# Rotating the first matmul's blocks over three PSUM banks, and giving the front turns a third bank

## The reference

```python
x = x + conv_ref(_ln_c(x), fc1_w, fc2_w, sa_w)     # channel gate, then a 7 x 7 spatial gate
t = _to_tokens(x)                                  # 192 tokens of 512 channels per image
t = t + ffn_ref(_ln_t(t), w1, w2)                  # 512 -> 2048 -> 512, both layers "bitlinear"
x = _from_tokens(t, x)

# conv_ref(v): ca = sigmoid(mlp(mean over pixels) + mlp(max over pixels)); v = v * ca
#              s = conv7x7([mean over channels, max over channels]);       return v * sigmoid(s)
# _bitlinear(x, w): w -> clip(round(w * rms), -1, 1) / rms;  x -> round(x * 127 / max|x|) / scale
#                   per token;  then x @ w.T
# ffn_ref: h = gelu(_bitlinear(x, w1)); out = _bitlinear(h, w2)
```

## Time and profile before

| | us |
|---|---|
| median of 3 runs | 321.71 (321.67, 321.71, 323.82) |
| the profiled execution | 321.15 |
| its span, first to last instruction | 319.4 |
| PE busy | 275.2 (86%) |
| DVE busy | 256.8 (80%) |
| ACT busy | 218.0 (68%) |
| POOL busy | 162.4 (51%) |

### The profile page before, as it was taken

The page is one execution under the profiler, slowest core; times in us unless marked ns, Lnnn a source line. Parts: engine busy times, 40 slices in busy tenths (PEclk is TensorE's granted clock), DMA queues, the critical chain, the costliest instruction groups (busy, mean ns, idle before and its releaser), DMA issues.

```text
span 319.4 us, 5840 instructions
## 1 busy us (share of the span) xinstructions
PE 275.2 (86%) x1834; PEld 153.2 (48%) x1834; DVE 256.8 (80%) x590; ACT 218.0 (68%) x442; POOL 162.4 (51%) x256
## 2 busy tenths in 40 slices
PE   3557659696899999999999999989999998899974
PEld 2444534543456355535553556455535553444431
DVE  1757979979698979897989798989997988799510
ACT  2286397578666878687868786858687757577731
POOL 7404355324855385538553855475538552455410
PEclk9999775959799999999999999999999999999999
DMA  4899400002373028402941294128402631263493
GB/s 132 315 382 422 131 1 2 0 0 43 26 167 66 12 57 232 99 19 49 240 92 27 39 230 102 34 36 222 109 19 49 165 69 23 45 164 67 79 218 99
DMA packets 71078, 34.20 MB, mean 107 GB/s; under 512 B 52040, under 2 KB 68424, under 8 KB 70536
## 3 DMA queue, kind: packets, MB, share of 16 engines
q1 hardware_dynamic: 69384, 32.78, 41.0%
q10 hardware_dynamic: 1664, 1.05, 1.2%
HBM read 14.94 MB, written 6.29 MB: 66 GB/s over the span
## 4 chain that ended last, share of the span: by engine, by line
PE 49%; DVE 27%; issue 9%; ACT 6%; POOL 4%; DMA 3%; SPq 1%; ACTq 0%; DVEq 0%; POOLq 0%
PE ps_o L1152 17%; PE ps_h L1141 9%; PE ps_t L1141 8%; DVE amax L842 4%; PE front L1074 3%; PE small L1117 3%; DVE t L815 3%; PE front L1161 2%; ACT junk L520 2%; PE ps_t L1183 2%; DVE st L817 2%; DVE amax L828 2%; DVE w_room L885 2%; DVE pv L782 2%; PE front L1126 1%
## 5 line engine op out<-in xcount | busy, mean ns | idle before, releaser
L1152 PE MATMUL ps_o<-w2T,hq 128*128 128x512 f16 x384 | 92.7, 380 | 1.2 <-DMA hq<-w_raw 1.2
L474 POOL TENSOR_SCALAR w_room<-w_room,q 128x1024 f32<-128x1024 f32 x48 | 59.0, 1241 | 54.6 <-DVE q L852 54.6
L842 DVE TENSOR_REDUCE amax<-w_room 128x1 f32<-128x1024 f32 (+1 forms) x48 | 57.1, 1208 | 2.2 <-ACT w_room L520 2.2
L1141 PE MATMUL ps_h<-w1T,xq 128*128 128x512 f16 x208 | 55.3, 412 | 1.0 <-ACT xq L520 1.0
L1152 PEld LDWEIGHTS ps_o<-w2T,hq 128*128 128x128 f16 x384 | 35.4, 98 | 37.3 <-issue 3.6
L520 ACT ACTIVATE w_raw<-w_room 128x1024 f16<-128x1024 f16 x48 | 50.1, 1048 | 0.6 <-POOL w_room L474 0.6
L520 ACT ACTIVATE w_room<-ps_h,s 128x512 f32<-128x512 f32 x52 | 35.1, 690 | 15.4 <-PE ps_h L1141 14.3
L1141 PE MATMUL ps_t<-w1T,xq 128*128 128x512 f16 x176 | 42.6, 379 | 0.0
L520 ACT ACTIVATE w_room<-ps_t,s 128x512 f32<-128x512 f32 x44 | 30.3, 688 | 7.7 <-PE ps_t L1141 7.6
L1141 PEld LDWEIGHTS ps_h<-w1T,xq 128*128 128x128 f16 x208 | 20.2, 105 | 25.1 <-issue 6.4
L520 ACT ACTIVATE junk_m<-front 128x192 bf16<-128x192 f32 x64 | 20.5, 331 | 16.2 <-DVE pooled L757 16.2
(11 more groups left out here) (125 smaller groups left out, 458.3 us busy)
## 6 DMA issues: line engine op xcount, KB each, us to landing
out<-w_room SPq DMA_DIRECT2D x16, 384.0 KB, 3.3
x_in<-in_x SPq DMA_DIRECT2D x14, 384.0 KB, 5.3
w_room<-in_L_ffn_w SPq DMA_DIRECT2D x4, 1024.0 KB, 8.9
w_raw<-in_L_ffn_w SPq DMA_DIRECT2D x4, 1024.0 KB, 12.1
x_in<-in_x ACTq DMA_DIRECT2D x2, 384.0 KB, 3.7
hq<-w_raw SPq DMA_TRANSPOSE x48, 3.2
fc_raw<-in_L_conv_fc_w ACTq DMA_DIRECT2D x2, 128.0 KB, 4.1
taps_rev<-in_L_conv_sa_w SPq DMA_DIRECT2D x2, 0.2 KB
```

Source lines behind the costliest of these rows:

```text
L474: pool.tensor_scalar(part, part, q2[tile.par][:, 0:1], MAGIC, ALU.mult, ALU.add).then_inc(g_rounded, 1)
L842: chain.mark(dve.tensor_reduce(amax2[:, i:i + 1], w1_room[:, first + i * F // 2:first + (i + 1) * F // 2 + i], AX.X, ALU.max, apply_absolu ...
L1141: last = pe.matmul(banks[b], xq[tile.pair.par][:, tile.s, k, :], w1T[:, k, b * 512:(b + 1) * 512], start=(k == 0), stop=(k == NC - 1))
L1152: last = pe.matmul(ps_o[:, :], hq[tile.par][:, k, :], w2T[:, k, :], start=(k == 0), stop=(k == NF - 1))
```

## The change

The four blocks of `ffn_in` go over three banks, `ps_h0`, `ps_h1` and `ps_t0`: the block with running number n = 4 * tile + b takes bank n % 3 (from tile 2 on; the first two tiles still use `ps_h0` and `ps_h1` alone). Block b of a tile now waits for `g_ready` of 4 * tile + b - 2, which is the gelu of three blocks earlier. For b = 3 this is the gelu of block 0 of the same tile. `ps_t1` becomes the third `front` bank. The lists `a` and `b` become `free[0]`, `free[1]`, `free[2]`, which carry over from round to round, and the tables say which of the three banks a turn takes. The order of the work on each engine stays as it was; what changes is the bank and the waits.

```diff
@@ -146,13 +146,18 @@
         ps_h = [pb(f"ps_h{i}", [P, 512]) for i in range(2)]
         ps_t = [pb(f"ps_t{i}", [P, 1024], f16) for i in range(2)]
         ps_o = pb("ps_o", [P, 512])
-        front = [pb(f"front{i}", [P, 512]) for i in range(2)]
+        front = [pb(f"front{i}", [P, 512])[:, :] for i in range(2)]
+        front.append(ps_t[1][:, :].bitcast(f32))
         small = pb("small", [P, 512])
-        front16 = [b[:, :].bitcast(f16) for b in front]
+        front16 = [b.bitcast(f16) for b in front]
         h_start = [ps_h[0][:, :], ps_h[1][:, :], ps_h[0][:, :], ps_h[1][:, :]]
-        h_loop = [ps_h[0][:, :], ps_h[1][:, :], ps_t[0][:, :].bitcast(f32), ps_t[1][:, :].bitcast(f32)]
+        h_loop = [ps_h[0][:, :], ps_h[1][:, :], ps_t[0][:, :].bitcast(f32)]
+
+        def h_bank(tile, b):
+
+            return h_start[b] if tile.at() < 2 else h_loop[tile.at(FB, b) % 3]
         fc1_ps = small[0:J, 16:20]
         fc2_ps = small[:, 32:32 + 2 * NC].rearrange("p (k i) -> p k i", i=2)
@@ -307,7 +312,7 @@
             return raw[:, 4 * i:4 * i + 4, :] if k == 0 else raw[:, i, :]
-        OUT_BANK, V1_BANK, XQ_BANK, X_BANK, CA_BANK = [0, 1, 0], [1, 0, 0, 0], [1, 1, 0], [0, 1, 1], [0, 1, 1]
+        OUT_BANK, V1_BANK, XQ_BANK, X_BANK, CA_BANK = [0, 2, 0], [1, 2, 1, 0], [0, 1, 2], [2, 0, 0], [1, 2, 1]
         def wait_all(eng, pairs):
             for semaphore, value in pairs:
                 wait(eng, semaphore, value)
...
@@ -564,14 +569,14 @@
                 copy(xq[tile.pair.par][:, tile.s, :, :],
                      front16[bank][:, 0:C].rearrange("p (k q) -> p k q", k=NC), xq_ready, bias=-F16_ZERO)
-            def gelu(tile, gate=None, banks=h_loop, blocks=range(FB)):
+            def gelu(tile, gate=None, blocks=range(FB)):
                 wait(act, s1_ready, tile.at(1, 1))
                 for b in blocks:
                     if b == 0 and gate:
                         gate_tokens(gate)
                     wait(act, h_done, tile.at(FB, b + 1))
-                    copy(g[tile.par][:, b * 512:(b + 1) * 512], banks[b], g_ready, ACT.Gelu,
+                    copy(g[tile.par][:, b * 512:(b + 1) * 512], h_bank(tile, b), g_ready, ACT.Gelu,
                          scale=s1[tile.pair.par][:, tile.s:tile.s + 1])
             def pack_g(tile, out_tile=None, out_bank=None, halves=range(2)):
...
@@ -1127,18 +1132,13 @@
                 last.then_inc(xq_turned, 1)
                 return [(xq_ready, tile.at(1, 1))]
-            def ffn_in(tile, banks=h_loop, blocks=range(FB)):
+            def ffn_in(tile, blocks=range(FB)):
                 wait(pe, xq_ready, tile.at(1, 1))
-
-                if banks is h_start:
-                    before = [-1, 0, 1, 2]
-                else:
-                    before = [-1, 0, 0, 0] if tile.at() == 2 else [-3, -2, -1, 0]
                 for b in blocks:
-                    wait(pe, g_ready, tile.at(FB, before[b]))
+                    wait(pe, g_ready, tile.at(FB, b - 1 if tile.at() < 2 else b - 2))
                     for k in range(NC):
-                        last = pe.matmul(banks[b], xq[tile.pair.par][:, tile.s, k, :],
+                        last = pe.matmul(h_bank(tile, b), xq[tile.pair.par][:, tile.s, k, :],
                                          w1T[:, k, b * 512:(b + 1) * 512], start=(k == 0), stop=(k == NC - 1))
                     last.then_inc(h_done, 1)
...
@@ -1270,49 +1270,61 @@
             a = turn_x(Tile(pair2, 2), 0, a)
             conv(pair1)
+            free = [a, b, []]
+
             def body(pair, attend, normalise, turn):
                 nxt, att, fresh = pair.plus(1), pair.plus(2), pair.plus(3)
-                a = [(xq_ready, pair.at(NT, NT))]
-                b = [(xt_ready, att.at(NT, NT))] if attend else [(scaled, NP * NT), (out_ready, pair.at(NT, -2))]
-                if attend:
-                    a = a + b
+                def res_out(tile, bank):
+                    free[bank] = turn_res(tile, bank, free[bank])
+
+                def channels(n):
+                    free[V1_BANK[n]] = turn_v1(att, n, V1_BANK[n], free[V1_BANK[n]])
+
+                def quantised(n):
+                    free[XQ_BANK[n]] = turn_xq(Tile(nxt, n), XQ_BANK[n], free[XQ_BANK[n]])
+
+                def tokens(n):
+                    free[X_BANK[n]] = turn_x(Tile(fresh, n), X_BANK[n], free[X_BANK[n]])
+
+                def gate(n):
+                    free[CA_BANK[n]] = spread_ca(Tile(att, n), CA_BANK[n], free[CA_BANK[n]])
                 ffn_in(Tile(pair, 2))
                 if pair.c > 0:
-                    a = turn_res(Tile(pair.plus(-1), 2), OUT_BANK[0], a)
-                if attend:
-                    b = turn_v1(att, 0, V1_BANK[0], b)
+                    res_out(Tile(pair.plus(-1), 2), OUT_BANK[0])
+                if attend:
+                    channels(0)
                 ffn_out(Tile(pair, 0), (0, 1))
                 if attend:
-                    a = turn_v1(att, 1, V1_BANK[1], a)
+                    channels(1)
                 ffn_out(Tile(pair, 0), (2,))
                 if normalise:
-                    b = turn_xq(Tile(nxt, 0), XQ_BANK[0], b)
+                    quantised(0)
                 ffn_out(Tile(pair, 0), (3,))
                 if attend:
-                    a = turn_v1(att, 2, V1_BANK[2], a)
+                    channels(2)
                 if normalise:
                     ffn_in(Tile(nxt, 0))
-                b = turn_res(Tile(pair, 0), OUT_BANK[1], b)
-                if attend:
-                    a = turn_v1(att, 3, V1_BANK[3], a)
+                res_out(Tile(pair, 0), OUT_BANK[1])
+                if attend:
+                    channels(3)
                 ffn_out(Tile(pair, 1), (0, 1))
                 ffn_out(Tile(pair, 1), (2,))
                 if normalise:
-                    b = turn_xq(Tile(nxt, 1), XQ_BANK[1], b)
+                    quantised(1)
                 if attend:
                     fc1(att)
                 ffn_out(Tile(pair, 1), (3,))
                 if attend:
                     if turn:
-                        a = turn_x(Tile(fresh, 0), X_BANK[0], a)
+                        tokens(0)
                     fc2(att)
                     if turn:
-                        b = turn_x(Tile(fresh, 1), X_BANK[1], b)
+                        tokens(1)
                 if normalise:
                     ffn_in(Tile(nxt, 1), blocks=(0, 1, 2))
@@ -1321,24 +1333,24 @@
                 if normalise:
                     ffn_in(Tile(nxt, 1), blocks=(3,))
                 if attend:
-                    a = spread_ca(Tile(att, 0), CA_BANK[0], a)
-                    b = spread_ca(Tile(att, 1), CA_BANK[1], b)
+                    gate(0)
+                    gate(1)
                 ffn_out(Tile(pair, 2), (0,))
-                a = turn_res(Tile(pair, 1), OUT_BANK[2], a)
-                if attend:
-                    b = spread_ca(Tile(att, 2), CA_BANK[2], b)
+                res_out(Tile(pair, 1), OUT_BANK[2])
+                if attend:
+                    gate(2)
                 ffn_out(Tile(pair, 2), (1, 2))
                 if normalise:
-                    a = turn_xq(Tile(nxt, 2), XQ_BANK[2], a)
+                    quantised(2)
                 ffn_out(Tile(pair, 2), (3,))
                 if turn:
-                    b = turn_x(Tile(fresh, 2), X_BANK[2], b)
+                    tokens(2)
                 if attend:
                     conv(att)
             for c in range(NP):
                 body(Pair(c), c < NP - 2, c < NP - 1, c < NP - 3)
-            turn_res(Tile(Pair(NP - 1), 2), OUT_BANK[0], [(out_ready, NP * NT - 1)])
+            turn_res(Tile(Pair(NP - 1), 2), OUT_BANK[0], free[OUT_BANK[0]])
 _INS = ["x", "L0_conv_fc1_w", "L0_conv_fc2_w", "L0_conv_sa_w", "L0_ffn_w1", "L0_ffn_w2"]
```

More of the change, by code:

```diff
@@ L525, in copy_x @@
                 wait(act, q1_ready, tile.at(1, 1 - 2 * NT))
-                copy(xt[tile.pair.par][:, tile.s, :], front[bank][:, :], xt_ready)
+                copy(xt[tile.pair.par][:, tile.s, :], front[bank], xt_ready)
             def token_mean(pair, k, bank):
@@ L594, in copy_out @@
                 copy(out_sb[tile.pair.par][:, :, tile_cols(tile.s)],
-                     front[bank][:, :].rearrange("p (k q) -> p k q", k=NC), out_ready)
+                     front[bank].rearrange("p (k q) -> p k q", k=NC), out_ready)
             def squares(k, raw, loaded, turns):
@@ L637, in _ @@
             squares(1, w2_raw, w2_loaded, (1,))
-            gelu(Tile(pair0, 0), None, h_start, (0, 1))
+            gelu(Tile(pair0, 0), None, (0, 1))
             token_mean(pair1, 1, 1)
             token_mean(pair1, 2, 0)
-            gelu(Tile(pair0, 0), None, h_start, (2, 3))
+            gelu(Tile(pair0, 0), None, (2, 3))
             copy_weights(1, (0,))
@@ L650, in _ @@
             sum_channels(Tile(pair1, 0))
-            gelu(Tile(pair0, 1), None, h_start, (0,))
+            gelu(Tile(pair0, 1), None, (0,))
             sum_channels(Tile(pair1, 1))
```

(20 more changed lines are left out.)

## The result

The changed kernel takes 325.73 us (median of 4 runs, 325.25 to 327.84), the kernel before, beside it, 322.49 us. The ratio is 1.0112 (95% interval 1.0072 to 1.0153). In a later series it was 1.0161 (1.0126 to 1.0195). Forecast were 320.9 us and a range up to 323.2. So the change makes the kernel slower by 1.1 to 1.6%, and the forecast was wrong in sign. Every ratio in this document leaves out runs more than 1.5% above the fastest of their kernel; that is one run, the one of 326.06 us under "Thin fill".

What follows compares the result with a forecast made beforehand. PE and DVE, both nearly full, were taken to bound each round in turn. The profiled 321.15 - 0.36 - 0.4 = 320.4 us; from the median, 321.71 - 0.8 = 320.9 us, range 319.2 to 323.2.

Steps and rivals of the forecast that it cites:

- The bound of a round: Each round is PE from `conv` to the second tile's `ffn_out`, then DVE until `conv`; `conv` stays at 176.42 in round 2.
- the stall that turns into another wait: At the ends of rounds 0 to 5, PE's wait for `copy_out` becomes a 0.9 us wait before `conv`; no gain.
- Three banks for the blocks cost nothing: In `ffn_in`, block 3 waits for its own tile's block 0 gelu, with 0.6 us spare at the tightest; cost 0.
- The 0.36 us of round 4: Mid-round 4, the rounded tile's turn no longer waits for a mean of ACT; gain 0.36 us, bounds 0 and 0.36.
- neither DVE nor POOL is waited for here: Reason given for taking the whole 0.36 us in round 4, nearest to the upper bound.
- The 0.4 us of round 5: In round 5 `res` is turned at once and DVE gets the third gate 0.6 us earlier; gain 0.4 us, bounds 0 and 0.6.
- The clock: Rival: TensorE's clock falls in one `ffn_in` per round, 16 matmuls, costing 20 us over 8 rounds, 341 us; chance 1%.
- 0 of 4.6 us: Value given to removing `turn_xq`'s six waits for `copy_out` at the ends of rounds 0 to 5, since DVE covers them.
- the 0.8 that was forecast: Total gain in us subtracted from the median of 321.71 us; its terms are 0.36 in round 4 and 0.4 in round 5.

Runs made afterwards that it cites:

- Thin fill: The changed kernel with 32 extra 3-column matmuls directly before the convolution of each round with attention; 322.72 us, ratio 1.0011.
- the kernel with that half alone: The kernel before with only the blocks of `ffn_in` moved to three banks, fourth bank unused, front turns on their two banks; 323.34 us, ratio 1.0015.
- the kernel with fill: The changed kernel with four 512-column matmuls, result never read, directly before the convolution of each round with attention; 322.19 us, ratio 0.9983.
- the stall moved without the banks: The kernel before, banks kept, with the turn of a round's last rounded tile moved behind the last quarter of `ffn_out`; 326.09 us, ratio 1.0118.
- the kernel with the stall moved: The kernel before, last rounded tile's turn moved behind `ffn_out`'s last quarter, here with four wide matmuls before the convolution; 321.86 us, ratio 0.9993.
- The kernel with one wait back: The changed kernel with PE again waiting for the output copy before turning a round's last rounded tile; 324.08 us, ratio 1.0048.
- the filled kernel before: The kernel before plus 3 wide matmuls before the last rounded tile's turn (rounds 0-5), 4 and 3 before convolutions of rounds 3 and 5; 321.88 us, ratio 0.9985.

## Why the prediction was wrong

**The bound of a round, and the stall that turns into another wait: right.** `conv` starts when DVE is through; rounds without a fall keep their length, and the wait for `split_stats` stands where it was forecast (about 0.9 us, measured 1.00 in rounds 0 and 1). What failed is the price of that wait, below.

**Three banks for the blocks cost nothing: right** as far as can be told, by the kernel with that half alone.

**The 0.36 us of round 4: the gain came and was given back.** In the kernel with fill, whose round 4 had no fall, `ffn_out`'s result is added at 227.71 and not at 228.11. DVE's timeline there, first this kernel, then the one before:

```profile
227.71 0.75 DVE L864 SCALAR_TENSOR_TENSOR res<-ps_o,s,t 128x512 f32<-128x512 f32 x1
228.38 1.16 DVE L820 SCALAR_TENSOR_TENSOR t<-pv,sg,xt 128x512 f32<-128x512 f32 x1
```

```profile
228.11 0.75 DVE L859 SCALAR_TENSOR_TENSOR res<-ps_o,s,t 128x512 f32<-128x512 f32 x1 [0.27 <-PE ps_o L1152]
228.77 0.81 DVE L815 SCALAR_TENSOR_TENSOR t<-pv,sg,xt 128x512 f32<-128x512 f32 x1
```

The next instruction takes 1.16 against 0.81 us, while POOL rounds in both. The round is 31.49 against 31.50 us. The step "neither DVE nor POOL is waited for here" failed: DVE, come earlier, met POOL's long instruction, and ends 1.66 us behind the start of POOL's work in the one trace and 1.65 in the other. That it is this encounter is read from the two traces and was not tried by itself.

**The 0.4 us of round 5: 0.2 us.** In the same kernel with fill, DVE got the third gate at 267.32 instead of 267.99, as forecast, and then waited 0.35 us for ACT's sum and met POOL's work twice (0.89 and 1.04 us, where two of the four instructions had been slow before). Within the bounds of 0 and 0.6.

**The clock: the step that failed.** The prediction put the wait that moves before `conv` into the sum as "0 of 4.6 us" and gave a fall of the clock 1%, because "longer stalls in one piece before `conv` speak for it, and the same total of stalls speaks against it", and because round 3 had kept its clock. The total alone is the wrong measure. In the kernel before, PE's idle time came in two parts with wide matmuls between them; the change put it in one part, next to the turns and to 1.1 us of 3-column matmuls. About the same sum in one place was followed by a fall in 8 of 18 rounds, shown both ways: the stall moved without the banks gives the loss, and fill at that place takes it away with the banks. The size was also wrong: the rival counted 16 slow matmuls in each of 8 rounds, 20 us. A fall lasts about 3.4 us and costs 1.4 to 1.7 us. Three of them make 4.5 us (1.51, 1.65 and 1.36 us, by the table, the last against the round of the kernel with fill); the spans differ by 4.8. Rounds 1 to 5 together are 4.2 us longer, and near the end of the kernel (at 314.84) PE waits 1.82 us for a transfer of `hq`, where it waited 1.19 before; why that is so is open. The Trainium skill, TensorE: Matmul & The Clock Gate, section A second HAM failure mode: psum-queue depth-cycling, tells of a clock that goes up and down where PE idles briefly between groups of matmuls. The trace of before did not show it, that of the changed kernel does, and the page deserved more than 1%.

**The gain behind it.** Where both kernels have their idle time filled, the change has 320.72 us and the kernel before 321.88, with intervals that don't overlap: 1.2 us, of the size of the 0.8 that was forecast. But the fills are not the same, and with four wide matmuls each, the change (322.19) and the kernel with the stall moved (321.86) show no such gain. So the gain isn't shown.

Open: in which rounds the clock falls. Two traces of the same kernel differ, and stalls of 1.00 us were followed by a fall in one round and not in another. The kernel with one wait back still loses half a per cent at the median; its profiled execution is its fastest run and has the one fall, so that the others are not explained. That the kernel before has falls in its slower runs is inferred from the narrower spread with fill.

## What to carry to other kernels

A wait that is moved to where another engine hides it is not free on TensorE: look at what lies next to it. In this kernel a stall of about 1 us in one piece beside thin matmuls was followed by a fall in a quarter of the places, one of about 2 us in most, at some 1.5 us per fall: give that a chance and a price where you see such a stall. Where PE must wait there, wide matmuls into a bank that is about to be overwritten are a cheap cure: in this kernel it turned a change that lost 1.1 to 1.6% into one that gains 0.5%.

## What the runs showed of the hardware

- Forty 3-column matmuls and 0.16 us of standing still ahead of the 42 thin ones of the convolution were followed by a fall (3.8 us with a mean clock of 0.55); with four to nine wide matmuls in these places no fall was seen in a window of 210 us of one trace.
- Early in the program the granted clock in the profile does not agree with the durations. In the filled kernel before, the window from 40 to 50 us says 1.00, and these four matmuls in it take 1.89 us, as long as in the kernel before, where they start at 46.93 and the window from 46.9 to 48.8 us says 0.50:

```profile
47.25 1.89 PE L1141 MATMUL ps_h<-w1T,xq 128*128 128x512 f16 x4 [0.87 <-ACT xq L520]
```

```profile
40.00:50.00 10.00, 7.48 (x45) 4.98 (x42) 7.90 (x14) 9.41 (x14) 4.81 (x9) 1.00 0.01 2
```

  So the mean clock of a whole run does not rank the runs: of the kernel before, some at 0.973 took 322.5 us and some at 0.951 took 321.2. The stretches of the rounds had to be read one by one.
